# Second layer between the halves of the next unit's first layer, in the expert stage of an attention and mixture-of-experts kernel

## The reference, cut to what matters

```python
x = x + _L0_xattn_ref(_layernorm(x), ctx_1024, ctx_1024, ...)
x = x + _L0_ffn_ref(_layernorm(x), router_w, w1, w2)

def _L0_ffn_ref(x, router_w, w1, w2):              # E = 8, K = 2, H = 1024
    probs = softmax(einsum('bsd,ed->bse', x, router_w))
    vals, idx = top_k(probs, K)
    for eid in range(e):
        w = sum(where(idx == eid, vals, 0), axis=-1)
        h = gelu(x_flat @ w1[eid].T, approximate=False)
        y = h @ w2[eid].T
        out = out + w[:, None] * y
```

## Time and profile before

| | us |
|---|---|
| median of three runs | 466.51 (464.68 to 468.06) |
| the profiled execution, its own time | 464.14 |
| its span in the trace | 462.3 |
| PE busy in it | 396.0 (86%) |
| DVE busy | 262.9 (57%) |
| ACT busy | 227.8 (49%) |
| POOL busy | 201.0 (43%) |

### The profile page before, as it was taken

How to read it: one execution, slowest core, us unless ns; L and a number is a source line. 1 busy time by engine, 2 the same in 40 slices (tenths; PEclk the granted TensorE clock), 3 DMA queues, 4 the chain that set the end, 5 groups by cost and what they waited for, 6 DMA issues and landing times.

```text
span 462.3 us, 8588 instructions
## 1 busy us (share of the span) xinstructions
PE 396.0 (86%) x2738; PEld 332.0 (72%) x2739; DVE 262.9 (57%) x592; ACT 227.8 (49%) x415; POOL 201.0 (43%) x183
## 2 busy tenths in 40 slices
PE   6967799999999996226899999999999999999930
PEld 2646665867766664213899999999999999999920
DVE  2898756646645223697648466464466868464300
ACT  1753656646546652410656556554467756554400
POOL 4946658553344222105216455445454353553221
PEclk9897999999999999557899999999999999999975
DMA  8345553362411011751545445343243752222221
GB/s 242 123 108 126 120 119 97 71 166 72 95 52 43 32 47 40 220 176 46 214 118 165 106 134 125 61 135 50 43 110 70 227 136 46 46 47 30 30 29 11
DMA packets 25719, 45.39 MB, mean 98 GB/s; under 512 B 6481, under 2 KB 19921, under 8 KB 22929
## 3 DMA queue, kind: packets, MB, share of 16 engines
q0 software_dynamic: 8448, 15.77, 19.1%
q1 hardware_dynamic: 13728, 26.32, 18.2%
q10 hardware_dynamic: 3504, 2.83, 2.0%
HBM read 31.52 MB, written 13.39 MB: 97 GB/s over the span
## 4 chain that ended last, share of the span: by engine, by line
PE 71%; DVE 9%; DMA 6%; issue 4%; POOL 4%; ACT 3%; SPq 0%; ACTq 0%; POOLq 0%; DVEq 0%
PE ps_s L1687 24%; PE ps_t L1704 14%; PE ps_t L1707 7%; PE ps_s L1364 3%; PE ps_t L1413 3%; DMA result<-big,rowtok 3%; PE ps_c L1669 2%; PE ps_c L1331 2%; DVE mx L965 2%; PE ps_a L1438 2%; PE ps_c L1438 2%; PE ps_a L1436 2%; PE ps_t L1410 2%; PE ps_c L1436 2%; PE ps_a L1464 1%
## 5 line engine op out<-in xcount | busy, mean ns | idle before, releaser
L1687 PE MATMUL ps_s<-xgT,KB 128*128 128x256 f32 x912 | 117.4, 285 | 2.7 <-DVE xgT L1248 1.5
L593 POOL DMA_INDIRECT result<-big,rowtok x38 | 66.9, 1761 | 112.0 <-DMA result<-big,rowtok 54.0
L1687 PEld LDWEIGHTS ps_s<-xgT,KB 128*128 128x128 f32 x912 | 112.1, 191 | 3.9 <-DVE xgT L1248 1.7
L965 DVE TENSOR_REDUCE mx<-ps_s 128x4 f32<-128x616 f32 x64 | 49.3, 797 | 30.7 <-PE ps_s L1364 30.5
L561 POOL DMA_INDIRECT big<-rows,gtok x38 | 42.4, 1115 | 43.8 <-DVE gtok L1225 23.8
L1704 PE MATMUL ps_t<-KB,HTb 128*128 x160 | 56.1, 394 | 0.0
L655 ACT ACTIVATE big<-ps_t 128x512 f32<-128x512 f32 x80 | 45.2, 593 | 21.0 <-PE ps_t L1413 18.0
L842 ACT ACTIVATE big<-ps_t,wrow 128x256 f32<-128x256 f32 x38 | 18.0, 475 | 69.9 <-PE ps_t L1707 69.9
L1704 PE MATMUL ps_t<-KB 128*128 x144 | 50.4, 394 | 0.0
L1291 DVE SCALAR_TENSOR_TENSOR big<-ps_t,wrow,big 128x256 f32<-128x256 f32 x38 | 18.3, 483 | 52.3 <-ACT big L842 49.1
L834 ACT ACTIVATE big<-ps_s 128x512 f32<-128x512 f32 x76 | 45.5, 598 | 0.0
(11 more groups left out here) (221 smaller groups left out, 678.8 us busy)
## 6 DMA issues: line engine op xcount, KB each, us to landing
VP<-in_wexp SPq DMA_DIRECT2D x8, 1024.0 KB, 6.0
big<-in_wexp SPq DMA_DIRECT2D x8, 1024.0 KB, 5.3
qd<-big SPq DMA_DIRECT2D x28, 128.0 KB, 2.3
KB<-qd POOLq DMA_DIRECT2D x7, 512.0 KB, 5.4
result<-x SPq DMA_DIRECT2D x8, 256.0 KB, 2.5
rows<-xn SPq DMA_DIRECT2D x8, 256.0 KB, 2.8
KB<-qd POOLq DMA_DIRECT2D x7, 256.0 KB, 6.0
XS<-in_x ACTq DMA_DIRECT2D x1, 1024.0 KB, 5.6
```

The source lines that it names most:

```text
L593: pool.indirect_dma_start(out, bass.IndirectOffsetOnAxis(rowtok[:, u, h:h + 1], 0), ys[:, 2 * (u % 2) + h, :], None, compute_op=ALU.add).t ...
L965: dve.tensor_reduce(mx[:, i, :, 2 * k:2 * k + 2].rearrange("p a b -> p b a"), ps_s[n % 2][:, :, 0:2 * KEYS].rearrange("p b (h k) -> p b h ...
L1687: last = mm(ps_s[j // 4][:, j // 2 % 2, (j % 2) * PAIR:(j % 2 + 1) * PAIR], w1[:, w, k, j * P:(j + 1) * P], xgT[:, u % 2, a, k, :], start= ...
```

## The change

Nothing is added or taken away in the computation. On PE, down(s) moves up by one place: it now stands between the two halves of up(s+1). On ACT and DVE the results of unit s move with it, in front of the last two quarters of unit s+1, and `split_w2` moves from behind the results to a place in front of them (on DVE behind take_rows).

```diff
@@ scalar: pair(s, u, i, has)
                 if has(1):
                     to_split = act.value_load(table(t_split, s + 1), min_val=0, max_val=E * E - 1)
-                    for h in range(2):
-                        with if_used(act, s + 1):
-                            gelu(s + 1, (u + 1) % 4, (2 * h, 2 * h + 1))
-                        with act.If(to_split % E > 0):
-                            split_w1(to_split % E, h)
+                    with if_used(act, s + 1):
+                        gelu(s + 1, (u + 1) % 4, (0, 1))
+                    with act.If(to_split % E > 0):
+                        split_w1(to_split % E, 0)
+                    with act.If(to_split >= E):
+                        e = to_split // E
+                        split_w2(e, e % 2)
                 for h in range(2):
                     scale_low(s, u, h)
                 if has(1):
-                    with act.If(to_split >= E):
-                        e = to_split // E
-                        split_w2(e, e % 2)
+                    with if_used(act, s + 1):
+                        gelu(s + 1, (u + 1) % 4, (2, 3))
+                    with act.If(to_split % E > 0):
+                        split_w1(to_split % E, 1)
@@ vector: pair(s, u, i, has)
-                    for h in range(2):
-                        with if_used(dve, s + 1):
-                            low_part(s + 1, (u + 1) % 4, (2 * h, 2 * h + 1))
-                        with dve.If(to_split % E > 0):
-                            split_w1(to_split % E, h)
-                        if h == 0 and has(2):
-                            with if_used(dve, s + 2):
-                                take_rows(s + 2, (u + 2) % 4, has(4))
+                    with if_used(dve, s + 1):
+                        low_part(s + 1, (u + 1) % 4, (0, 1))
+                    with dve.If(to_split % E > 0):
+                        split_w1(to_split % E, 0)
+                    if has(2):
+                        with if_used(dve, s + 2):
+                            take_rows(s + 2, (u + 2) % 4, has(4))
+                    with dve.If(to_split >= E):
+                        e = to_split // E
+                        split_w2(e, e % 2)
                 for h in range(2):
                     dve.wait_ge(low_made, 2 * s + h + 1)
...
                 if has(1):
-                    with dve.If(to_split >= E):
-                        e = to_split // E
-                        split_w2(e, e % 2)
+                    with if_used(dve, s + 1):
+                        low_part(s + 1, (u + 1) % 4, (2, 3))
+                    with dve.If(to_split % E > 0):
+                        split_w1(to_split % E, 1)
@@ tensor: pair(s, u, i, has)
                         if has(2):
                             with if_used(pe, s + 2):
                                 row_transposes(s + 2, (u + 2) % 4)
+                down(s, u, e0)
+                if has(1):
+                    with if_used(pe, s + 1):
                         up(s + 1, (u + 1) % 4, e1, 1)
-                down(s, u, e0)
```

## The result

Over 20 runs of each kernel the changed one takes 464.29 us, the one before 467.91 us; the ratio is 0.9945, with a 95% interval of 0.9920 to 0.9971. The ratio is taken over the runs within 1.5% of the fastest of their kernel, so it is not the quotient of the two medians. On 467.9 us that is 2.6 us less (1.4 to 3.7), where 2.83 were forecast; the medians are 3.6 us apart. Single runs of the changed kernel spread over 7.6 us and those of the kernel before over 11.3, and the profiled execution of the changed kernel is one of its longer ones: 467.95 us, with a span of 466.1 against 462.3. So the two spans say nothing by themselves. Part of the difference lies ahead of all code that changed: the transposes of unit 0 start at 215.59 us before and at 220.86 after.

A forecast was written before the change was run, and what follows sets the result against it. PE's matmuls were taken to bound the stage up to down(17)'s first half, then serial scatters. Middle 0 and end -2.83 us took the 466.51 us median to 463.7 us, range 461.0 to 467.4.

The forecast's parts named there:

- The lower bound by the steps: Steps between the last scatters, 3 x 4.66 to 3 x 5.01 us, giving -0.5 to +0.6 us; the low end was 462.9.
- The end, -2.83 us: End of the stage: down(17) starts at 429.12 instead of 431.95, and four serial scatters move with it, 2.83 us earlier.
- POOL free in time: Unit 16's second scatter lets go of POOL at 431.5, 1.7 us before down(17)'s first scatter.
- The place with a margin of 0.2 us: Seventh step of down(18), directly behind up(18, half 1): last low part ready at 439.35, wanted at 439.58.
- The middle, 0: Steady periods between units 3 and 18: same PE work in another order, still 11.65 us per unit, no gain or loss.
- my list of the waits: PE's possible waits in the middle: low parts, split weights, scatters before ys is reused, tests; none expected to delay PE.
- the fullest period: The period in which pair(10) runs, with both kinds of split because units 11 and 12 each begin an expert.
- P+9.9: Forecast end of DVE's moved second-weights split, 9.9 us after P, when PE starts up(s+1, half 0).
- Margins of the low parts and of the second weights: At the second layer: low parts 4.2 and 3.5 us early; second weights' margin grows from 1.1 to 5.0 us.
- The end follows PE: Rival at the stage's end: PE's unmoved last matmul decides, not the scatters; gain 0, 466.5 us; chance 0.12.
- Slower, because the second layer waits for low parts: Rival at each down(s)'s seventh step: 0.5 us of wait in each of 17 units gives 472 us; chance 0.07.
- More than the end: Rival: 2 us more gained in 216 to 251 us or by shorter scatters, time 461; chance 0.06.

## Why the prediction was right

**The number and the mechanism.** 463.7 us were forecast for the median and 464.29 measured, 2.83 us less were forecast and 2.6 measured by the ratio. The hit is in part luck: the kernel before came out at 467.91 and not 466.51 in more runs, and in the profiles the stage is only 1.63 us shorter. The end came about as worked out and the middle did not. (The lower bound by the steps, 463.7 - 0.5, is 463.2, not the 462.9 that I gave.)

**The end, -2.83 us.** Measured -2.82 in the profile, -2.81 with the new order at the end alone. The step that carries the forecast, down(17) one half earlier and four scatters in series behind it, held in every part: the steps of 4.70 to 4.88 us against 4.66 to 5.01, the chain leaving PE after the first half of down(17), POOL free in time. The place with a margin of 0.2 us was tighter than worked out, and harmless. PE goes from unit 18's first layer into down(18) without a gap, and the last quarter's low part is ready at 445.88. PE's rows, with the seventh step at 446.02, and DVE's row of that low part:

```profile
441.15 2.88 PE L1693 MATMUL ps_s<-xgT,KB 128*128 128x256 f32 x24
443.87 0.39 PE L1710 MATMUL ps_t<-KB,HTb 128*128 x1
...
445.88 0.28 PE L1713 MATMUL ps_t<-KB,HTb 128*128 x1
446.02 0.49 PE L1710 MATMUL ps_t<-KB,HTb 128*128 x1
```

```profile
445.19 0.69 DVE L1267 TENSOR_TENSOR HTb<-big,HTb 128x512 fp32r<-128x512 f32 x1 [0.62 <-ACT big L834]
```

The first matmul of the seventh step takes 0.49 us where its neighbours take 0.40, so by these rows the margin was about used up and some 0.1 us went there. The row of waits has no entry for it, and the scatters hid it.

**The middle, 0.** I had written that the forecast is wrong if PE shows idle time in the middle. It does, so this part of the forecast failed. That PE "loses only if some wait now ends late" was right, and my list of the waits was short by one. The net of 1.19 us in one profile hides two terms that I did not have. The first is the wait at unit 14. Of the queues that the split is moved past I followed ACT, DVE and PE, and of POOL only the scatters' landing back to `ys`; I left out the gathers that stand behind those scatters, and who waits for them. In the fullest period the split ended at P+10.8 and not P+9.9 (take_rows ended 0.4 us later, and DVE then took 0.54 us to cross the tests, for which I had nothing); the results came 2 us later than with the split behind them, and with them the gathers. I also passed over the loads that come some 7 us earlier, since I asked only whether they come in time for the split, and not what they lie beside. The middle is 2.25 us longer than with the split behind the results. Of these 1.57 stand in the period with the wait (13.10 us against 11.53); the other 0.7 are slower periods behind it, 11.90, 11.64 and 11.75 us where the other kernel has 11.53 or 11.54, at a granted clock of 1.00, and their cause is open. The second term is the 11.53 us per unit, -1.06 us over the stretch with the split behind. Neither was in my sum, and by chance the second takes back about half of the first.

**Margins of the low parts and of the second weights.** But for the 0.1 us above PE never waited for either in the changed kernel. That the split had to move was right in sign and weak in size: I gave the margin before as 1.1 us and the new one as 5.0, but did not price the case without the move, which is 32 us in the middle.

**The rivals.** "The end follows PE" did not come about with accumulating scatters. The transfers took 3.76 to 4.01 us; the 2.3 us that I had estimated from the Trainium skill's page "DMA: Bandwidth & Descriptors", section "Anatomy of one DMA — SWDGE (gpsimd) path", was not reached even by plain scatters, at 2.55, 2.58, 3.04 and 4.22 us. "Slower, because the second layer waits for low parts" did not come about. "More than the end" had a true core, the faster periods, in a place where I had excluded a gain, because I took "PE is busy all the time" for "PE cannot be faster".

## What to carry to other kernels

Where a busy engine hands over to a serial chain of transfers at the end, moving the last handover forward gives its full length as long as the chain stays the later of the two (2.8 us here), while the same move in the steady middle, where PE waits for nothing, has no wait to take away and cost 1.19 us here: make it first where the chain starts. When a step is moved, follow every queue behind it to its end, the transfers that its semaphores set off included, and ask what these will lie beside. A wait of PE can cost more than its length. Here the waits of 1.41 and 1.50 us left the granted clock at 1.00. The seven of 2.49 to 3.73 us made the stretch 32.2 us longer for 20.8 us of waits, and the one of 4.03 us cost 6.9, with the clock at the 1.2 GHz level behind all of these but one. Two waits were 2.82 us long, and only one of them was followed by the lower clock, so here the length of a wait alone did not decide it.

## What was not expected of the hardware

First-layer matmuls of the same shape run in two paces at full granted clock: 48 of them in 5.44 or in 5.66 us by the chain of waits, 113 and 118 ns each. In the order of before nearly all halves take 2.83 us. With the split behind the results most groups of 48 in the loop take 5.44, and the second layer 5.65 where it took 5.55, for a sum of 11.53 against 11.65. In the changed kernel six of the ten groups ahead of the wait at unit 14 do; the five behind it all take 5.65 or 5.66. Which of the two a group gets also changes from kernel to kernel for the last unit (5.66 before, 5.65 after, 5.44 with the new order at the end alone), so what decides it stays open.

The issue of the second gather takes 2.06 us on POOL in the changed kernel, 0.99 with the split behind. In the former it lies beside the DVE split of second weights (369.28 to 371.57 us), which reads two operands from SBUF, and starts while that runs. The Trainium skill, "SBUF — State Buffer", section "SBUF: two separate sides", says that such a DVE operation and a GpSimd operation that reads SBUF exclude each other. The row agrees with that. So do the others: of the 38 gather issues of the changed kernel, the 20 that start while no DVE operation with two operands from SBUF runs take 0.94 to 1.02 us, the one at 369.05 among them, beside which the split starts only 0.23 us later; all 14 that take over 1.1 us start inside such an operation. The four others start inside one too and take no longer than 1.02. In the kernel before it is the same, with 20 issues of 0.95 to 1.03 us outside and all 13 long ones inside. No run changes that operation alone, so other causes are not excluded.
